# Block diagonals by transfers instead of by engine writes in a perceiver layer, and TensorE's head scores two units later

## The reference

```python
scores = jnp.einsum('bqd,bkd->bqk', Q, K) / jnp.sqrt(jnp.float32(d))
p = jax.nn.softmax(scores, axis=-1)
...
sh = _ln(jax.nn.silu(x1) * x2, s_ln_g, s_ln_b)
shared_out = jnp.einsum('bth,dh->btd', sh, sw3) + sb3
```

## Time and profile before

| what | value |
|---|---|
| median of 3 runs | 1451.5 us (1449.05 to 1451.91) |
| span of the profiled execution (no other time of it is given) | 1452.8 us |
| TensorE busy | 1365.6 us, 94% |
| VectorE busy | 1128.1 us, 78% |
| ScalarE, GpSimd busy | 601.9 us (41%), 526.1 us (36%) |
| mean transfer rate | 139 GB/s, 38.3% of the 16 engines on SyncE's queue |

### The profile page before, as it was taken

One profiled execution on the slowest core, in us unless ns is written; L12 is line 12 of the kernel. 1 busy time (PEld: TensorE's weight loads), 2 busy tenths in 40 slices (PEclk: granted clock), 3 DMA queues, 4 the chain that ended last, 5 costly groups with the idle time before them and its releaser, 6 DMA issues.

```text
span 1452.8 us, 33270 instructions
## 1 busy us (share of the span) xinstructions
PE 1365.6 (94%) x13860; PEld 851.7 (59%) x13861; DVE 1128.1 (78%) x2335; ACT 601.9 (41%) x1147; POOL 526.1 (36%) x545
## 2 busy tenths in 40 slices
PE   7679999999999999999999999999999999998888
PEld 3355566666656666665665656666665666655443
DVE  6787777777787877778778877777778877777776
ACT  2544444443444444343434444444444444443222
POOL 0133333433444333443443333343443433343222
PEclk9899999999999999999999999999999999999899
DMA  9732444433333444433333344443333344434440
GB/s 349 259 131 74 146 146 146 144 123 105 133 112 115 146 146 146 146 137 101 122 130 105 139 146 146 146 142 114 111 138 105 123 146 146 147 134 161 149 161 30
DMA packets 38662, 201.41 MB, mean 139 GB/s; under 512 B 5096, under 2 KB 5992, under 8 KB 28400
## 3 DMA queue, kind: packets, MB, share of 16 engines
q1 hardware_dynamic: 37648, 198.93, 38.3%
q10 hardware_dynamic: 864, 0.36, 0.1%
HBM read 182.24 MB, written 17.04 MB: 137 GB/s over the span
## 4 chain that ended last, share of the span: by engine, by line
PE 70%; DVE 19%; POOL 4%; ACT 4%; issue 3%; DMA 0%; DVEq 0%; POOLq 0%; ACTq 0%; SPq 0%
PE ps_a L1716 11%; PE ps_a L1739 8%; PE ps_t L1739 7%; PE ps_t L1703 6%; PE ps_a L1725 6%; PE ps_a L1751 4%; PE ps_a L1783 4%; POOL rstd L636 4%; PE ps_t L1716 3%; PE ps_v L1716 3%; DVE stats L1178 3%; DVE arena L1309 3%; PE ps_t L1826 2%; PE ps_t L1775 2%; PE ps_t L1751 2%
## 5 line engine op out<-in xcount | busy, mean ns | idle before, releaser
L645 POOL TENSOR_TENSOR act_l<-act_t,act_h 128x512 f16<-128x512 f32 (+1 forms) x176 | 199.5, 1134 | 351.4 <-ACT act_t L789 199.4
L636 POOL TENSOR_TENSOR rstd<-var,mhalf 128x1 f32<-128x1 f32 x224 | 181.8, 812 | 333.7 <-DVE var L1180 328.9
L781 ACT ACTIVATE act_h<-ps_t,scale 128x512 f16<-128x512 f32 (+1 forms) x110 | 70.8, 644 | 206.2 <-PE ps_t L1703 206.2
L645 POOL TENSOR_TENSOR last_slot<-last_slot 128x512 f16<-128x512 f32 x80 | 90.0, 1125 | 156.7 <-ACT last_slot L789 90.8
L1739 PE MATMUL ps_a<-act_h,arena 128*128 128x128 f16 x1408 | 87.6, 221 | 17.3 <-ACT act_h L781 17.3
L1739 PEld LDWEIGHTS ps_a<-act_h,arena 128*128 128x128 f16 x1408 | 81.9, 99 | 28.3 <-ACT act_h L781 21.3
L789 ACT ACTIVATE act_t<-ps_t,scale 128x512 f32<-128x512 f32 (+1 forms) x110 | 70.3, 639 | 49.1 <-PE ps_t L1703 49.1
L1739 PE MATMUL ps_t<-act_h,arena 128*128 128x128 f16 x1408 | 87.0, 221 | 3.3 <-ACT act_h L781 3.3
L1716 PE MATMUL ps_a<-arena,act_h 128*128 128x512 f16 x352 | 83.6, 380 | 1.9 <-ACT act_h L781 1.9
L1309 DVE TENSOR_SCALAR arena<-ps_a,unscale 32x512 f32<-32x512 f32 x64 | 48.2, 753 | 47.0 <-PE ps_a L1751 45.8
L1739 PEld LDWEIGHTS ps_t<-act_h,arena 128*128 128x128 f16 x1408 | 81.4, 99 | 4.9 <-DVE arena L1037 2.4
(11 more groups left out here) (380 smaller groups left out, 3150.7 us busy)
## 6 DMA issues: line engine op xcount, KB each, us to landing
arena<-in_ctx_t SPq DMA_DIRECT2D x32, 2056.0 KB, 8.4
arena<-in_ctx_n SPq DMA_DIRECT2D x32, 2048.0 KB
ctx_last<-in_ctx_last SPq DMA_DIRECT2D x32, 256.0 KB
arena<-in_ew SPq DMA_DIRECT2D x8, 1024.0 KB, 6.3
x_in<-in_x SPq DMA_DIRECT2D x22, 256.0 KB, 7.3
x_scratch<-rows SPq DMA_DIRECT2D x22, 256.0 KB, 8.8
out<-rows SPq DMA_DIRECT2D x22, 256.0 KB, 2.1
arena<-in_ew SPq DMA_DIRECT2D x8, 512.0 KB, 7.2
```

Source lines behind the costliest of these rows:

```text
L636: nc.gpsimd.tensor_tensor(rstd[s][:], var[s][:], mhalf[:], ALU.pow).then_inc(rstd_ready[s], 1)
L645: nc.gpsimd.tensor_tensor(act_l[s][:, chunks], act_t[s][:, chunks], act_h[s][:, chunks], ALU.subtract).then_inc(act_l_ready[s], 1)
L781: nc.scalar.activation(act_h[s][:, 0:width // P].rearrange("p c r -> p (c r)"), bank[s][:, 0:width], ACT.Copy, scale=scale[:, k:k + 1]).th ...
```

## The change

Both block diagonals are filled by transfers. ScalarE copies the whole K product into rows3 (project_k), and SyncE moves its four quarters to kbd (heads_k, lag 2, new in LOADS ahead of store_x2). VectorE turns the head weights by one transpose of 128 partitions into rows3, and SyncE moves four quarters to pbd (heads_p, after load_ctx_n). VectorE's project_k is gone. kbd and pbd have another order inside, so that a transfer writes whole rows and TensorE reads each operand in four runs of 32 words.

VectorE turns the self-attention's weights (turn_p, between context_norm and self_mix), 32 x 32 blocks at a time, since off the diagonal they are zero; TensorE's and ScalarE's turn_p are gone. GpSimd adds b3 to x2 (x2_bias, between turn_z and xn_moments), once x2 is stored, and VectorE's ffn_out is one operation that waits for it. The scale of the scores is folded into earlier factors, and some waits of VectorE on itself move from an operation's end to the place that needs it. On TensorE in ORDER alone, head_scores stands behind turn_xn and project_v.

```diff
 ORDER = {
     "pe": [(2, "project_q"), (3, "turn_z"), (2, "project_k_l"), (3, "ffn_out"), (3, "ffn_out_l"), (1, "turn_pc"),
-        (2, "project_q_l"), (1, "context_mix"), (2, "head_scores"), (0, "turn_xn"), (2, "project_v"),
+        (2, "project_q_l"), (1, "context_mix"), (0, "turn_xn"), (2, "project_v"), (2, "head_scores"),
...
-    "pool": [(3, "silu"), (3, "turn_z"), (0, "xn_moments"), (0, "turn_xn"), (2, "head_scores"), (1, "turn_w"),
+    "pool": [(3, "silu"), (3, "turn_z"), (3, "x2_bias"), (0, "xn_moments"), (0, "turn_xn"), (2, "head_scores"), (1, "turn_w"),
...
-LOADS = [(0, "load_x"), (0, "set_first"), (0, "set_rest"), (0, "load_ctx_t"),
+LOADS = [(0, "load_x"), (0, "set_first"), (0, "set_rest"), (0, "load_ctx_t"), (2, "heads_k"),
          (3, "store_x2"), (1, "e_first"), (1, "e_second"), (1, "e_rows"), (2, "e_fifth"), (3, "store"),
-         (0, "load_ctx_n"), (1, "e_third"), (1, "e_fourth"), (2, "e_sixth")]
+         (0, "load_ctx_n"), (2, "heads_p"), (1, "e_third"), (1, "e_fourth"), (2, "e_sixth")]
...
+                def heads_k(s, r, tile):
+                    sp.wait_ge(k_out, tile + 1)
...
+                    for h in range(HPC):
+                        mine = slice(HD * h, HD * (h + 1))
+                        sp.dma_start(kbd[mine, h, :, :, :].rearrange("p c g k -> p (c g k)"), rows3[s][mine, :]
+                                     ).then_inc(k_ready, 16)
+
+                def heads_p(s, r, tile):
+                    sp.wait_ge(heads_turned, tile + 1)
...
+                    for g in range(G):
+                        mine = slice(T * g, T * (g + 1))
+                        sp.dma_start(pbd[mine, g, :, :].rearrange("p h q -> p (h q)"), rows3[s][mine, :]
+                                     ).then_inc(pbd_ready, 16)
...
+                def x2_bias(s, r, tile):
+                    pool.wait_ge(rows_ready[s], 6 * r + 5)
+                    pool.wait_ge(x2_stored[s], 16 * r + 32)
...
+                    nc.gpsimd.tensor_tensor(rows3[s][:], rows3[s][:], b3[:], ALU.add).then_inc(x2_biased, 1)
...
-                    for h in (0, 1):
-                        rows = slice(HD * h, HD * (h + 1))
-                        nc.scalar.activation(kbd[rows, :, :, h, :],
-                                             ps_a[s][rows, :].rearrange("p (c g k) -> p c g k", c=C, g=G), ACT.Copy,
-                                             scale=unscale[rows, K_WATTN:K_WATTN + 1]).then_inc(k_ready[s], 1)
+                    nc.scalar.activation(rows3[s][:], ps_a[s][:], ACT.Copy, scale=unscale[:, K_WATTN:K_WATTN + 1]
+                                         ).then_inc(k_out, 1)
...
+                def turn_p(s, r, tile):
+                    chain = Chain("turn_p", s, r)
+                    dve.wait_ge(p_ready[s], 3 * r + 1)
+                    nc.vector.transpose(p_t[s][:, 0:P], p_n[s][:, 0:P]).then_inc(p_t_ready[s], 1)
+                    chain.last(nc.vector.reciprocal(inv[s][:, 0:1], total[s][:, 0:1]))
...
                 def ffn_out(s, r, tile):
                     dve.wait_ge(rows_done[s], 6 * r + 6)
-                    chain = Chain("ffn_out", s, r)
-                    chain(nc.vector.scalar_tensor_tensor(rows2[s][:], ps_a[s][:], unscale[:, K_W3:K_W3 + 1], b3[:],
-                                                         ALU.mult, ALU.add))
-                    nc.vector.tensor_tensor(rows2[s][:], rows2[s][:], rows3[s][:], ALU.add).then_inc(out_ready[s], 1)
-                    chain.end()
+                    dve.wait_ge(x2_biased, tile + 1)
+                    nc.vector.scalar_tensor_tensor(rows2[s][:], ps_a[s][:], unscale[:, K_W3:K_W3 + 1], rows3[s][:],
+                                                   ALU.mult, ALU.add).then_inc(out_ready[s], 1)
```

More of the change, by code:

```diff
@@ L146 @@
         (1, "e_gate_c"), (1, "e_bias0"), (2, "e_bias3"), (0, "self_scores"), (2, "e_z3"), (1, "e_z0"),
-        (1, "context_out"), (0, "self_mix")],
+        (1, "context_out"), (0, "turn_p"), (0, "self_mix")],
     "act": [(3, "head_mix_t"), (3, "head_mix"), (2, "turn_h2"), (2, "turn_h2_t"), (2, "e_zt0"), (2, "e_gate1"),
@@ L160 @@
 }
-LOADS = [(0, "load_x"), (0, "set_first"), (0, "set_rest"), (0, "load_ctx_t"),
+LOADS = [(0, "load_x"), (0, "set_first"), (0, "set_rest"), (0, "load_ctx_t"), (2, "heads_k"),
          (3, "store_x2"), (1, "e_first"), (1, "e_second"), (1, "e_rows"), (2, "e_fifth"), (3, "store"),
-         (0, "load_ctx_n"), (1, "e_third"), (1, "e_fourth"), (2, "e_sixth")]
-STEPS = {"xn_moments": 2, "self_scores": 2, "self_mix": 5, "context_scores": 1, "context_scaled": 2, "context_out": 4, "hidden": 5,
-         "out_norm": 3, "head_scores": 2, "head_total": 1, "head_weights": 1, "project_out": 2, "ffn_in": 1, "silu": 4, "ffn_out": 1}
+         (0, "load_ctx_n"), (2, "heads_p"), (1, "e_third"), (1, "e_fourth"), (2, "e_sixth")]
+STEPS = {"xn_moments": 2, "self_scores": 1, "turn_p": 1, "self_mix": 4, "context_scaled": 2, "context_out": 4, "hidden": 5,
+         "out_norm": 3, "head_scores": 2, "head_total": 1, "head_weights": 1, "project_out": 2, "ffn_in": 1, "silu": 4}
 FIRST_ROUNDS, LAST_FROM = 4, -2
@@ L670, in _ @@
                     "turn_z": remainder(8, H),
-                    "head_scores": head_scores, "set_1": set_1, "set_2": set_2,
+                    "head_scores": head_scores, "x2_bias": x2_bias, "set_1": set_1, "set_2": set_2,
                     "e_norm": expert_std(1), **{f"e_zn{k}": expert_std(k + 2) for k in range(EH)}})
@@ L820, in self_scores @@
                     act.wait_ge(ntop_ready[s], 2 * r + 1)
-                    nc.scalar.activation(p_n[s][:, 0:P], rows3[s][:, 0:P], ACT.Exp, bias=ntop[s][:], scale=XSCALE,
+                    nc.scalar.activation(p_n[s][:, 0:P], rows3[s][:, 0:P], ACT.Exp, bias=ntop[s][:],
                                          accum_out=total[s][:, 0:1]).then_inc(p_ready[s], 1)
-                def turn_p(s, r, tile):
-                    act.wait_ge(p_turned[s], 2 * r + 1)
-                    nc.scalar.copy(p_t[s][:, 0:P], ps_a[s][:, 0:P]).then_inc(p_t_ready[s], 1)
                 def project_query(s, r, tile):
@@ L1222, in self_mix @@
                     chain = Chain("self_mix", s, r)
[L1223 to L1224 removed]
                     dve.wait_ge(rows_done[s], 6 * r + 1)
+                    made_by("turn_p", s, r)
                     dve.wait_ge(out_stored[s], 16 * r + 16)
@@ L1270, in context_out @@
                     moments(chain, s, rows3[s][:], 1e-3)
-                    chain(scaled(s, rows1[s][:], rows3[s][:], gamma[:]))
+                    chain.last(scaled(s, rows1[s][:], rows3[s][:], gamma[:]))
                     chain.end()
                 def context_norm(s, r, tile):
-                    offset(s, r, 3, rows1[s][:], beta[:]).then_inc(rows_ready[s], 1)
+                    offset(s, r, 3, rows1[s][:], beta[:], "context_out").then_inc(rows_ready[s], 1)
                 def hidden(s, r, tile):
@@ L1285, in hidden @@
                     moments(chain, s, rows3[s][:], 1e-3)
-                    chain(scaled(s, rows2[s][:], rows3[s][:], gamma[:]))
+                    chain.last(scaled(s, rows2[s][:], rows3[s][:], gamma[:]))
                     chain.end()
@@ L1290, in out_norm @@
                     chain = Chain("out_norm", s, r)
-                    chain(offset(s, r, 4, rows2[s][:], beta[:]))
+                    chain(offset(s, r, 4, rows2[s][:], beta[:], "hidden"))
                     nc.vector.scalar_tensor_tensor(rows2[s][:], rows2[s][:], 0.0, x_in[s][:], ALU.max, ALU.add
@@ L1341, in head_weights @@
                     dve.wait_ge(decayed[s], r + 1)
-                    if tile == 0:
-                        dve.wait_ge(consts_ready, 5)
-                    else:
-                        dve.wait_ge(y_done[(s - 1) % SLOTN], r + (s > 0))
                     chain(nc.vector.tensor_tensor(by_head(rows1[s][:]), sc, per_head(inv[s][:]), ALU.mult))
-                    for g in range(G):
-                        rows = slice(T * g, T * (g + 1))
-                        nc.vector.transpose(pbd[rows, :, g, :], by_head(rows1[s][rows, :])).then_inc(pbd_ready[s], 1)
+                    nc.vector.transpose(sc, by_head(rows1[s][:])).then_inc(heads_turned, 1)
                     chain.end()
@@ L1766, in self_scores @@
                     mm.then_inc(scored[s], 1)
-                def turn_p(s, r, tile):
-                    pe.wait_ge(p_ready[s], 3 * r + 1)
-                    nc.tensor.transpose(ps_a[s][:, 0:P], p_n[s][:, 0:P], ident[:]).then_inc(p_turned[s], 1)
                 def self_mix(s, r, tile):
```

129 lines of the change are left out of this document (63 added, 66 removed), and 1 row of the table FIRST.

## The result

The changed kernel takes 1844.4 us (median of 4 runs, 1843.0 to 1846.3) against 1451.7 for the kernel before: 1.2716 times as long, 95% interval 1.2696 to 1.2735. The forecast was 1718, the range ended at 1805. The direction and both waits were right; the size was short by 126 us. Three executions further down, one each of e5, e9 and e11, took 3545, 6950 and 3553 us for a reason that no run shows, and the times given leave them out.

What follows compares the result with a forecast made beforehand. The prediction took TensorE's queue as the bound. Its steps summed to 8.75 us a round, times 26 = 227, plus 39 at the ends, on a span of 1452.8: 1719, forecast as 1718 us; own range 1685 to 1755, wider range 1650 to 1805.

Steps and rivals of the forecast that it cites:

- step 1: TensorE's turned rows start 3.9 us later a round, since x2_bias and then ffn_out wait for x2's late store.
- step 2: TensorE's head scores behind the value product: +1.0 us a round out of the chain's shadow, +2.05 second wait ahead of turn_w.
- step 3: Self-attention weights turned on VectorE: -0.2 us a round for TensorE's dropped turn, +0.5 waiting for VectorE's turn_p.
- step 4: Granted clock falls behind TensorE's first wait, slowing the work after it: +1.5 us a round, bounds 0 and 3.0.
- (b): Rival: second clock fall, landing one microsecond longer, half a microsecond more in step 3; 11.75 a round, 1802 us; chance 0.20.
- The ends: Rounds outside the 26 steady ones: round 3, rounds 30 and 31, late expert loads, round 33; together 39 us.
- (a): Rival: the same TensorE waits at full clock, 7.25 us a round more, 1674 us; chance 0.12.
- (c): Rival: x2's store lands in time, so a round grows by only 2.3 us, 1512 us; chance 0.08.
- (d): Rival: faster, the shorter VectorE chain hiding everything if scores are read early enough; 1440 us; chance 0.03.

Runs made afterwards that it cites:

- e5: The kernel before, with only TensorE's head scores moved behind the value product in the steady rounds; 1548.3 us.
- e9: The changed kernel with 24 products that nobody reads in TensorE's first wait only, the second wait left empty; 1792.1 us.
- e11: The changed kernel with SyncE issuing the store of x2 between two and two of the four K blocks; 1796.7 us.
- e4: The changed kernel with both TensorE waits filled with products that nobody reads, 24 ahead of the turned rows and 8 ahead of turn_w; 1761.6 us.
- e13: The changed kernel with only TensorE's first wait filled with unread products, a repeat of e9 to get its profile; 1794.0 us.
- e14: The changed kernel with 8 products that nobody reads in the second wait only, ahead of turn_w, the first left empty; 1803.4 us.
- e6: The changed kernel with VectorE's context_mix and context_scaled, and ScalarE's context_scaled, ahead of the head scores; 1755.0 us.
- e7: The changed kernel with the store of x2 ahead of the context load and VectorE's context_mix ahead of its head scores; 1532.2 us.
- e8: The changed kernel with the store of x2 ahead of the context load and TensorE's head scores back ahead of the turned rows; 1526.3 us.
- e12: The changed kernel with the first expert tile's loads ahead of the K blocks and e_third ahead of the weight blocks; 1829.1 us.
- e2: The changed kernel with SyncE's store of x2 ahead of the 2 MB context load, K blocks in place; 1593.7 us.

## Why the prediction came out short

The mechanism was the forecast's, wait by wait; sizes were off, one of them by more than a factor of two. The terms of a round, forecast and measured:

| term | forecast | measured | from |
|---|---|---|---|
| step 1, late turned rows | 3.9 | 5.1 | 7.94, the mean of the 26 rounds, less 2.86 |
| step 2, head scores | 1.0 | 1.0 | e5 |
| step 2, second wait | 2.05 | 2.04 | wait ahead of turn_w |
| step 3 | 0.3 | 0.25 | 0.46 less the 0.2 of the turn |
| step 4, clock | 1.5 | 3.6 | from the turned rows to the next context mix, 45.06 on average, less 41.46 in e4's filled rounds |
| not in the sum | 0 | 0.4 | what is left |
| round | 8.75 | 12.4 | 52.99 less 40.63 |

The 0.4 is no further wait. From start to start the second wait and self_mix's take 0.2 more than their idle times, and two hand-overs between products (to the head scores, to the head mix) take 0.1 more each, as the timelines of e4 and of the kernel before show.

**Step 4 failed first.** Its mechanism (a fall behind the waits) stands by e4, e13 and e14, the size does not. The prediction took 1.47 us from one product of the opening and charged it once. In the round shown above the low clock covers all of the turned rows, the value product and most of the head scores, 807.30 to 813.11 = 5.81 us where e4 needs 3.3, and a second fall comes behind turn_w, which stood only in the bounds and in rival (b). On average that is 2.1 us a round too little, 55 us in 26 rounds.

**Step 1 was 1.2 short, 31 us.** The block issues stand 0.6 apart, not 0.38 and 0.48: those rows were issues of other shapes, and none showed a transfer between two on-chip tiles. This gives 0.6 of the 1.2 (e11 confirms 0.6 an issue), the landing gives 0.2, GpSimd's add 0.1. Another 0.1 is the mean of four rounds in which the turned rows start 8.35 to 9.06 us behind the mix instead of 7.8; why, no run shows.

**Steps 2 and 3 held.** The second wait was forecast at 2.05 and is 2.02 to 2.04 in every run that has it unfilled; e6 and e7 show that VectorE's order was its cause. Step 3's half microsecond was there, but it had been picked between 0 and 1.8, so that it came so close is luck. Two terms priced at 0 held as well: the head scores take 1.08 us with the new blocks (e8's row) as with the old (e5's), so reading in four runs of 32 words cost nothing, and the head mix of the round shown (L1830) does not wait for the weight blocks.

**The ends were 31 us short** (70 against 39). The opening took 18.7 where the prediction had 4 for round 3; there TensorE waits 8.25 us ahead of the turned rows of one tile. Rounds 30 and 31 took 16.8 for 11, the tail 34.1 for 24. e12 shows 15 us of the tail; the rest of it, and the opening, were not taken apart.

Of the rivals, (b) came nearest, with its second fall; its landing of one microsecond more did not come. (a), the same waits at full clock, is e4: 1762 and not 1674, by the ends (38 us), by step 1 (1.4 a round in e4) and by another 0.5 a round. (c), the store in time, is e2: it had 2.3 us a round, and e2 measures 3.5, mostly because the turned rows start 2.66 us behind the mix there and not at 1.8, with x2_bias still in the way. The order alone, in e5, costs 3.3, and 3.7 with the longer rounds. (d) is out: no run with any part of the change is faster than before.

The range was too narrow for a reason that can be named. Its upper end was (b), which took a second fall, 1.0 more in the store's path, half a microsecond more in step 3 and 45 us at the ends. What lay above that is 25 us at the ends (70, not 45) and 0.6 a round, 16 us, as much as the clock's 3.6 lies above its bound of 3.0.

## What to carry to other kernels

A wait of TensorE cost more than its length here: price the work behind each wait at the lower clock too, and for every wait of the round, with full clock as the other bound. When a change makes something wait for a store, look at what stands ahead of that store in its queue, before looking at the transfer; one issue moved up gave back 251 of 393 us here. And price an issue from a row of its own shape, or give it a bound that is twice as wide.

## What the runs showed of the hardware

Issuing a 64 KB transfer from 32 partitions of one on-chip tile to another took SyncE 0.6 us, where the issues of the earlier trace rows stand 0.38 and 0.48 apart; it lands in 2.0 us. Products that nobody reads made a kernel 83 us faster: the granted clock behind its waits read 1.00 (e4) instead of 0.55 and 0.69. A 2.03 us wait of TensorE brings the clock down in some rounds and not in others of the same program (four of 26 in e2, every fourth in e5, 18 of 25 in e13), and no run here tells which.
